# Layer 1 attention: a batch's probabilities split in one slot, keys and queries scaled on the scalar engine

## What is computed

```python
x = L0_attn_hidden_states
x = _layernorm(x + _L0_attn_ref(...))   # linear attention
x = _layernorm(x + _L0_ffn_ref(...))    # low-rank experts
x = _layernorm(x + _L1_attn_ref(...))   # softmax attention, the part changed here
x = _layernorm(x + _L1_ffn_ref(...))    # dequantised MLP
```

```python
q = rmsnorm((x @ Wq + bq).reshape(b, n, H, HD), gq)
k = rmsnorm((x @ Wk + bk).reshape(b, n, H, HD), gk)
v = (x @ Wv + bv).reshape(b, n, H, HD)
scores = jnp.einsum('bnhd,bmhd->bhnm', q, k) / np.sqrt(HD)
attn = softmax(scores)
out = jnp.einsum('bhnm,bmhd->bnhd', attn, v).reshape(b, n, H * HD)
return out @ Wo + bo
```

## Time and profile before

| | |
|---|---|
| median of 3 runs | 3316.5 us (3315.22 to 3330.63) |
| the profiled execution | 3324.06 us |
| its span, first to last instruction | 3322.2 us |
| PE busy | 2993.8 us (90%) |
| DVE busy | 2018.2 us (61%) |
| POOL busy | 1582.9 us (48%) |
| ACT busy | 1346.1 us (41%) |
| mean granted clock of TensorE | 0.985 of full speed |

### The profile page before, as it was taken

How to read it: one execution, slowest core, us unless ns; L and a number is a source line. 1 busy time by engine, 2 the same in 40 slices (tenths; PEclk the granted TensorE clock), 3 DMA queues, 4 the chain that set the end, 5 groups by cost and what they waited for, 6 DMA issues and landing times. The chain is left out here.

```text
span 3322.2 us, 57041 instructions
## 1 busy us (share of the span) xinstructions
PE 2993.8 (90%) x17632; PEld 2684.5 (81%) x17632; DVE 2018.2 (61%) x3189; ACT 1346.1 (41%) x2375; POOL 1582.9 (48%) x1075
## 2 busy tenths in 40 slices
PE   7999999999999887888888888888888888886998
PEld 7989999899899767778787788888887888875786
DVE  3445544544455557666677666677776677774555
ACT  3333333333333223445444544454444454443221
POOL 3333333333333413555555555555555555553765
PEclk9999999999999989999999999999999999998999
DMA  4121121211111111334343434343343343334551
GB/s 126 52 60 56 57 59 49 60 58 51 60 55 53 29 36 54 99 96 105 94 105 95 105 95 105 95 106 98 99 104 87 95 105 97 101 88 131 153 142 54
DMA packets 225483, 279.66 MB, mean 84 GB/s; under 512 B 48256, under 2 KB 124048, under 8 KB 225296
## 3 DMA queue, kind: packets, MB, share of 16 engines
q1 hardware_dynamic: 224576, 278.11, 31.5%
q10 hardware_dynamic: 816, 0.79, 0.1%
q0 software_dynamic: 32, 0.02, 0.0%
HBM read 125.63 MB, written 2.10 MB: 38 GB/s over the span
## 5 line engine op out<-in xcount | busy, mean ns | idle before, releaser
L1343 ACT ACTIVATE b_prob<-b_s_ps,b_shift 128x1024 f32<-128x1024 f32 x256 | 285.9, 1117 | 562.9 <-DVE b_shift L1491 562.9
L1281 POOL TENSOR_TENSOR pT_lo<-pT_lo,pT_hi 128x1024 fp32r<-128x1024 f32 x128 | 305.2, 2385 | 166.7 <-ACT pT_hi L1338 166.7
L1281 POOL TENSOR_TENSOR b_pT_lo<-b_pT_lo,b_pT_hi 128x1024 fp32r<-128x1024 f32 x128 | 304.9, 2383 | 160.7 <-ACT b_pT_hi L1338 160.7
L82 PE MATMUL b_pj_kq<-b_w_hi,xT_hi 128*128 128x384 f32 x1008 | 346.1, 343 | 8.5 <-DVE b_nat L1461 8.5
L83 PE MATMUL b_pj_kq<-b_w_lo,xT_hi 128*128 128x384 f32 x1008 | 344.1, 341 | 0.0
L84 PE MATMUL b_pj_kq<-b_w_hi,xT_lo 128*128 128x384 f32 x1008 | 344.1, 341 | 0.0
L1499 DVE STREAM_TRANSPOSE b_blocks<-b_prob 128x1024 f32<-128x1024 f32 x256 | 316.3, 1235 | 2.6 <-ACT b_prob L1343 2.6
L506 ACT ACTIVATE a_sig<-a_pj 128x512 f32<-128x512 f32 x192 | 115.1, 600 | 485.8 <-PE a_pj L84 485.8
L82 PE MATMUL a_pj<-b_w_hi,xT_hi 128*128 128x256 f32 x1024 | 295.3, 288 | 12.6 <-DVE xT_lo L647 11.6
L1491 DVE TENSOR_REDUCE b_shift<-b_s_ps 128x1 f32<-128x1024 f32 x256 | 303.7, 1187 | 2.7 <-PE b_s_ps L84 2.7
L84 PE MATMUL a_pj<-b_w_hi,xT_lo 128*128 128x256 f32 x1024 | 289.6, 283 | 0.0
(11 more groups left out here) (257 smaller groups left out, 8948.4 us busy)
## 6 DMA issues: line engine op xcount, KB each, us to landing
pT_lo<-b_blocks SPq DMA_DIRECT2D x1024, 64.0 KB, 2.0
b_pT_lo<-b_blocks SPq DMA_DIRECT2D x1024, 64.0 KB, 2.0
b_w_raw<-in_w SPq DMA_DIRECT2D x32, 768.0 KB, 4.4
b_w_raw<-in_w SPq DMA_DIRECT2D x95, 256.0 KB, 3.2
a_k_raw<-a_k_blocks SPq DMA_DIRECT2D x512, 32.0 KB, 1.8
a_w_raw<-in_w SPq DMA_DIRECT2D x32, 256.0 KB, 2.6
a_ow_raw<-in_ow SPq DMA_DIRECT2D x32, 256.0 KB, 3.1
b_ow_raw<-in_ow SPq DMA_DIRECT2D x32, 256.0 KB, 2.7
```

What stands on the lines that cost most here:

```text
L82: pe.matmul(out, w_hi, x_hi, start=first, stop=False)
L1281: pool.tensor_tensor(pT_lo[i % 2][:, :, cut, :], f(pT_lo[i % 2][:, :, cut, :]), f(pT_hi[i % 2][:, :, cut, :]), ALU.subtract).then_inc(pT_l ...
L1343: act.activation(prob[t % 2][:, :], s_ps[t % 2][:, :], ACT.Exp, bias=shift[:, t:t + 1], accum_out=row_sum[:, t:t + 1]).then_inc(exp_done, 1)
```

## The change

`split_part` becomes `split_batch`: ACT and POOL now do both halves of a batch in its even slot, one right behind the other, and nothing of it in the odd slot. `scale_kq` moves from VectorE, where it was one multiply of 128x512 with a broadcast operand, to ScalarE, where it is four copies of 128x128 with a per-partition scale, between the copies of the probabilities and the exponential of the even slots. The number of transfers and of matmuls and their order stay. Line numbers behind L1184 move by 1 to 14.

```diff
-        def split_part(h, cur, rest, s):
-
-            n = (s - 4) % 8
+        def split_batch(h, cur, rest, s):
+
+            if s % 2:
+                return None
             if s >= 4:
-                return (h, n // 2, n % 2) if cur else None
-            return (h - 1, n // 2, n % 2) if rest else None
+                return (h, (s - 4) // 2) if cur else None
+            return (h - 1, (s + 4) // 2) if rest else None
...
-                    if split_part(h, cur, rest, s):
-                        prob_lo(*split_part(h, cur, rest, s))
+                    if split_batch(h, cur, rest, s):
+                        for part in range(2):
+                            prob_lo(*split_batch(h, cur, rest, s), part)
...
+            def scale_kq(g, bg, i):
+
+                act.wait_ge(rstd_ready, NB * g + i + 1)
+                for u in range(BATCH):
+                    for k in range(2):
+                        part = nat[i][:, u, k * HD:(k + 1) * HD]
+                        last = act.activation(part, part, ACT.Copy, scale=rstd[bg][:, BATCH * i + u, k:k + 1])
+                last.then_inc(kq_scaled, 1)
...
-                    if split_part(h, cur, rest, s):
-                        prob_hi(*split_part(h, cur, rest, s))
+                    if split_batch(h, cur, rest, s):
+                        for part in range(2):
+                            prob_hi(*split_batch(h, cur, rest, s), part)
+                    if nxt and s % 2 == 0:
+                        scale_kq(h + 1, 1 - b, s // 2)
...
-            def scale_kq(g, bg, i):
-                dve.wait_ge(rstd_ready, NB * g + i + 1)
-                both = nat[i][:, :, 0:2 * HD].rearrange("p t (k d) -> p t k d", k=2)
-                dve.tensor_tensor(both, both, rstd[bg][:, BATCH * i:BATCH * (i + 1), :].unsqueeze(3).broadcast_to(
-                    [P, BATCH, 2, HD]), ALU.mult).then_inc(kq_scaled, 1)
...
-                    if nxt and s % 2 == 0:
-                        scale_kq(h + 1, 1 - b, s // 2)
```

## The result

The changed kernel takes 3191.7 us (median of 4 runs, 3188.1 to 3192.9), the kernel before 3322.7 with one more run beside it (3315.2 to 3330.6): a ratio of 0.9604, interval 0.9574 to 0.9633. That is 131 us against the median with the fourth run, 125 us against the 3316.5 that stood ahead of the prediction; the four runs of the kernel before lie in two groups, 3315.2 and 3316.5, 3328.8 and 3330.6, so that one more run moves their median. Forecast were 129 us and 3188 us.

A forecast was written before the change was run, and what follows sets the result against it. The bound was taken to be a chain through POOL's late second-half subtraction, 54.5 us a head. At 50.2 after, 4.3 us over 30.5 heads gives 131, less 2 is 129 us: 3316.5 to 3188 us, range 3140 to 3217.

The forecast's parts named there:

- D: Start of ACT's first-half copy in an even slot, released by the last of 16 transfers; exponential forecast 3.1 us later.
- D to X: From D over ACT's queue to VectorE's block transpose (X): 11.9 us, plus 0.52 for each weight copy.
- X to D: From VectorE's block transpose to the D one pair later, over 16 transfers issued by SP: 12.70 us.
- T: TensorE's transposes in the odd slot, forecast to wait for ACT's scalings until D + 3.25, about 0.9 us a pair.
- the loop: D to D by way of X, spanning two slot pairs: 24.6 us plus 0.52 for each weight copy.
- V0: TensorE's products of a batch's first half, said to need POOL's first subtraction at D + 3.6.
- Rival (a): TensorE becomes the bound and all its 221.6 us of idle time is recovered: 3095 us; chance 0.10.
- Rival (b): Loads in SP's queue delay the move, X to D grows by 1 us per pair: 3246 us; chance 0.12.
- Rival (c): ACT's first scaling stalls on POOL's power (reciprocal roots), holding up ACT's queue: 3393 us; chance 0.08.
- Rival (d): Another 2 us wait replaces TensorE's, needing scaling copies of 0.8 us instead of 0.29: 3316 us; chance 0.04.
- the 2 us for the last head: Taken off the saving: the second copy stands unhidden ahead of three exponentials there, 0.96 us each at most.
- the 30.5 heads: Heads the loop runs for, first head's middle to last but one, at 4.3 us saved each: 131 us.

The follow-up runs named there:

- edit one alone: Both halves' copy and subtraction in the even slot, scaling left as one VectorE multiply between `take` and `out_lo`, against the kernel before: 3227.5 us, ratio 0.9711.
- The second edit: Scaling as four ACT copies ahead of the exponential instead of VectorE's multiply; alone, with the halves in two slots, against the kernel before: 3239.5 us, ratio 0.9752.

## Why the prediction was right, and where it was not

The bound of the kernel before was read rightly, and so was what takes its place. Step by step: both copies 1.92 us (1.92 measured); the scaling 0.39 us (0.386), the exponential at D + 3.1 (3.11); D to X 12.9 with two weight copies (12.99); X to D 12.70 (12.72); T at D + 3.25 (2014.85 to 2018.08, 3.23); a head 50.2 us (50.4); the sum 129 us (125 against the median it was stated for). T's wait was put at 0.9 us a pair and is 0.75. POOL is off the path: no wait of TensorE for it is left. Halving the move and leaving out two scalings confirm both halves of the loop and its span of two pairs. Two slips bear on nothing: by its own terms the lower end of the forecast's range is 3147 - 12 = 3135, not 3140, and V0 comes at D + 3.25 + 2.53 = D + 5.8, not at D + 3.6.

Rival (a), TensorE as the bound, needed a shorter move, and the run with half a move shows that this was the right condition; the other that the prediction set, scalings nearly free, was not needed: they were all in that run. Rival (b): the loads in SP's queue cost nothing, X to D stays at 12.7 to 12.9. Rival (c): the power was in time, 0.95 to 2.2 us ahead of the first scaling in the three pairs looked at (forecast 1.3); ACT never waits for it. Rival (d): the scalings cost 0.386 us, not 0.8.

One step failed, outside the sum: "With edit one alone, as that rule would have it, [...] some 30 us faster than I forecast". It is 36 us slower than the changed kernel. The step took the multiply at its 0.60 us and left out what the multiply waits for. By the Trainium skill, "ScalarE: Activation LUTs", section "Rules for kernel authors", the multiply belonged on VectorE; the runs agree only if it is placed right: 3227, 3190 or 3206 us on VectorE, by its place alone, 3192 us on ACT. What ACT's form buys is that the multiply's 0.60 us leave VectorE's queue and that ACT's queue reaches the scalings when the power is done. The second edit is therefore worth 36 us on top of the first (3227.5 less 3191.7, from two series), and I had counted it as a loss of 30.

Not tested were the 2 us for the last head, nor the 30.5 heads as such.

## What to carry to other kernels

When a wait goes, redo the sum for everything that had been covered by it: here POOL's power of 1 us was hidden under a wait for TensorE, and cost some 72 us once that wait was gone, of which a swap of two instructions gave back 37. In a loop over engines and a transfer, count how many rounds it spans before pricing an instruction on it: one that spans two rounds gives back half. And before moving an operation to an idle moment of its own engine, look at what the neighbour engine does in that moment.

## What the runs showed of the hardware

- Some instructions of VectorE and POOL's subtractions shut each other out for whole instructions: a 0.69 us multiply of two SBUF tiles took 2.50 us beside POOL's subtraction, and 128x128 multiplies by a per-partition scalar 934 ns on average. Others were not slowed: the block transpose, also from SBUF to SBUF, took 1.23 us beside POOL's weight subtraction (2025.95, POOL's from 2025.67 to 2026.97, first edit alone), and `add_output` 0.73 us inside a subtraction of POOL's in the kernel before (2031.95, POOL's from 2030.02 to 2032.37). ACT's copies from and to SBUF did not suffer (386 ns).
- TensorE's granted clock stayed at 1.00 with waits of up to 1.67 us, once in about 50 us, in the changed kernel, and was 0.54 over the 3 us behind the start of the transposes that had waited 2.14 us in the run with four more copies. That run came out 57 us above the 71 expected; the clock's share of it was not measured by itself, since the exponential's waits for the row maximum grew as well.
- The length of the wait alone did not decide it. In the kernel before, TensorE waits 1.4 to 2.0 us in every pair and the granted clock is 1.00, except from 2500 to 2550 us, where it is 0.86 to 0.93. The first of these rows stands ahead of that stretch, the second at its start: the wait is the same, the product behind it is longer.

```profile
2400.69 0.39 PE L82 MATMUL b_o_ps<-b_pT_hi,b_v_hi 128*128 128x256 f32 x1 [2.00 <-POOL b_pT_lo L1281]
...
2509.82 0.58 PE L82 MATMUL b_o_ps<-b_pT_hi,b_v_hi 128*128 128x256 f32 x1 [2.01 <-POOL b_pT_lo L1281]
```

Over the kernel before's 26 runs beside the experiments, the 14 of 3313 to 3318 us show mean granted clocks of 0.984 to 0.987, the others, up to 3343 us, 0.981 to 0.985.
